# Cross attention and a mixture of experts on one core: two batches normed together at the start, a shorter tile table, and new instruction orders

## What is computed

```python
def _L0_xattn_ref(q, k, v):                       # q: (16, 128, 256), k = v: (16, 128, 64)
    qh = q.reshape(B, S, KV, G, D).transpose(0, 2, 3, 1, 4)
    ...
    scores = jnp.einsum('bkgsd,bktd->bkgst', qh, kh) / scale
    weights = jax.nn.softmax(scores, axis=-1)
    out = jnp.einsum('bkgst,bktd->bkgsd', weights, vh)
...
def _L0_ffn_ref(x, gate_w, w1, w2, w3):
    scores = jnp.einsum('ti,ei->te', xt, gate_w)
    probs = jax.nn.softmax(scores, axis=-1)
    expert_weights, expert_indices = jax.lax.top_k(probs, NUM_ACT)
    expert_weights = expert_weights / expert_weights.sum(axis=-1, keepdims=True)
    x1 = jax.nn.silu(jnp.einsum('ti,eoi->teo', xt, w1))
    x3 = jnp.einsum('ti,eoi->teo', xt, w3)
    expert_outs_all = jnp.einsum('teo,eio->tei', x1 * x3, w2)
    ...
x = x + _L0_xattn_ref(_layernorm(x, axis=-1), ctx_512, ctx_512)
x = x + _L0_ffn_ref(_layernorm(x, axis=-1), gate_w, w1, w2, w3)
```

## Time and profile before

| | |
|---|---|
| three executions | 444.84, 445.28 and 445.86 us, median 445.28 |
| the profiled execution | 443.68 us, of it the span 441.8 us |
| granted TensorE clock, mean | 0.943 of full speed |
| busy TensorE / VectorE / ScalarE / POOL | 355.9 / 233.6 / 196.7 / 183.6 us |
| moved by DMA | 51.16 MB, 116 GB/s over the span |
| chain that ended last | TensorE 53%, DMA 16%, VectorE 8%, issue 8%, POOL 8% |

### The profile page before, as it was taken

One profiled execution on the slowest core, in us unless ns is written; L12 is line 12 of the kernel. 1 busy time (PEld: TensorE's weight loads), 2 busy tenths in 40 slices (PEclk: granted clock), 3 DMA queues, 4 the chain that ended last, 5 costly groups with the idle time before them and its releaser, 6 DMA issues.

```text
span 441.8 us, 8620 instructions
## 1 busy us (share of the span) xinstructions
PE 355.9 (81%) x2255; PEld 255.9 (58%) x2256; DVE 233.6 (53%) x659; ACT 196.7 (45%) x397; POOL 183.6 (42%) x361
## 2 busy tenths in 40 slices
PE   0177878798888879833059999999999999999991
PEld 0054444455445445222038888888888888888870
DVE  6777786888787776558943222233232222333320
ACT  3325768686777657859022223222222332322220
POOL 6662263377655746476301232322222332222232
PEclk9989999999999998975559999999999999999997
DMA  6676798968876785853412333333333333333222
GB/s 204 148 156 128 216 222 202 225 151 208 202 180 183 185 218 165 282 170 107 144 48 37 61 50 49 48 50 57 48 51 57 48 48 48 52 54 48 36 24 24
DMA packets 46209, 51.16 MB, mean 116 GB/s; under 512 B 18659, under 2 KB 39267, under 8 KB 46179
## 3 DMA queue, kind: packets, MB, share of 16 engines
q1 hardware_dynamic: 37299, 39.64, 35.3%
q0 software_dynamic: 7152, 9.34, 13.5%
q10 hardware_dynamic: 1728, 1.82, 1.3%
HBM read 31.51 MB, written 16.69 MB: 109 GB/s over the span
## 4 chain that ended last, share of the span: by engine, by line
PE 53%; DMA 16%; DVE 8%; issue 8%; POOL 8%; SPq 3%; ACT 2%; POOLq 1%; ACTq 0%
PE bank L898 25%; PE bank L916 15%; DMA qst<-negT 10%; PE bank L908 4%; DVE wlo L1306 3%; POOL slots_d L545 3%; DMA rows<-rows 2%; PE bank L886 2%; PE bank L720 2%; PE bank L697 1%; SPq L315 1%; DMA qst<-qparts_d 1%; PE bank L694 1%; POOL x L516 1%; PE bank L733 1%
## 5 line engine op out<-in xcount | busy, mean ns | idle before, releaser
L660 POOL DMA_INDIRECT out_rows<-ys,meta x39 | 60.9, 1561 | 155.6 <-DVE ys L1537 145.3
L1251 DVE TENSOR_REDUCE negm<-bank 128x4 f32<-128x512 f32 x128 | 83.9, 680 | 25.0 <-PE bank L697 23.5
L1530 DVE TENSOR_TENSOR gat<-bank,sil 128x512 f32<-128x512 f32 x39 | 27.0, 692 | 112.8 <-PE bank L898 112.8
L967 ACT ACTIVATE prob<-bank 128x512 f32<-128x512 f32 x128 | 73.1, 597 | 26.7 <-PE bank L720 23.6
L916 PE MATMUL bank<-w,gT 128*128 x312 | 73.9, 380 | 0.8 <-ACT gT L1171 0.8
L1165 ACT ACTIVATE sil<-bank 128x512 f32<-128x512 f32 x39 | 23.3, 597 | 105.9 <-PE bank L898 105.9
L720 PE MATMUL bank<-qst,kst 128*128 128x512 bf16 x128 | 49.0, 387 | 20.8 <-DMA qst<-negT 18.8
L898 PE MATMUL bank<-whi,xhi 128*128 x156 | 60.3, 468 | 1.2 <-ACT xhi L1159 1.2
L916 PEld LDWEIGHTS bank<-w,gT 128*128 128x128 f32 x312 | 56.3, 190 | 7.1 <-issue 1.0
L697 PEld LDWEIGHTS bank<-kst,qst 125*128 125x128 bf16 x512 | 41.5, 102 | 23.3 <-issue 2.8
L697 PE MATMUL bank<-kst,qst 125*128 125x128 bf16 x512 | 51.8, 227 | 0.0
(11 more groups left out here) (121 smaller groups left out, 474.5 us busy)
## 6 DMA issues: line engine op xcount, KB each, us to landing
xs<-slots_d SPq DMA_DIRECT2D x39, 129.0 KB, 2.0
w<-in_w1T SPq DMA_DIRECT2D x8, 512.0 KB
w<-in_w3T SPq DMA_DIRECT2D x8, 512.0 KB
w<-in_w2T SPq DMA_DIRECT2D x8, 512.0 KB
qparts_d<-qp SPq DMA_DIRECT2D x16, 192.0 KB, 4.9
qst<-qparts_d SPq DMA_DIRECT2D x16, 192.0 KB
qst<-qparts_d SPq DMA_DIRECT2D x16, 128.0 KB
vblk<-in_v SPq DMA_DIRECT2D x16, 128.0 KB
```

What stands on the lines that cost most here:

```text
L660: pool.indirect_dma_start(out, IndirectOffsetOnAxis(ap=meta[:, r4, 0:1].bitcast(I32), axis=0), ys[:, r4, :], None, compute_op=ALU.add).the ...
L967: act.activation(prob[:, k, :], ps_e[k % 2][:, :], ACT.Exp, scale=SCALE).then_inc(exp_done, 1)
L1251: dve.tensor_reduce(negm[:, b % 2, g * G:(g + 1) * G], ps_s[(8 * b + g) % 3][:, :].rearrange("p (h t) -> p h t", h=G), AX.X, ALU.max, nega ...
L1530: dve.tensor_tensor(gat[:, u, :], ps_h3[u][:, :], sil, ALU.mult).then_inc(g_done, 1)
```

## The change

- `GROUPS` becomes (0, 2), (2, 4), (4, 8), (8, 12), (12, 16): batches 0 and 1 share the first root, of two columns.
- The table of tiles counts in rows in place of tiles. It has 12 steps: two steps of 39 columns are gone and one of 8 columns is new. `row0` is ready two steps before the end, and SP waits for it alone (`ROW0`); ScalarE does not wait for the table any more.
- `place(8)` is ahead of the table instead of behind it.
- The spare padding (two DMAs) is sent by SP in round -1.
- The first score group of a batch goes out one slot earlier, at the end of the round before.
- All steps of all engines stand in new orders. Of these: `neg_transpose` goes behind the fourth exponent product (and in odd rounds behind `pv`); `root_unit` goes from the head of odd rounds to the end of even ones on POOL; `normal1` of odd rounds' ends goes to even rounds on ScalarE; w2 is loaded in rounds 14 and 15 (two pieces each) and after the loop (four), before two in each of rounds 12 to 15; POOL forms remainder 5 instead of 2.

```diff
-GROUPS = [(0, 1), (1, 4), (4, 8), (8, 12), (12, 16)]
+GROUPS = [(0, 2), (2, 4), (4, 8), (8, 12), (12, 16)]
...
-    c[:, C_TILE:C_TILE + NT] = np.arange(NT)
+    c[:, C_TILE:C_TILE + NT] = np.arange(NT) * P
...
+            def pad_spare():
+                sp.wait_ge(pad_row, 3)
+                sp.dma_start(out[T:T + P, :], pad[:, 0:D]).then_inc(pads_out, 16)
+                sp.dma_start(slots_d[E * REGION:E * REGION + P, :], pad[:, :]).then_inc(pads_out, 16)
...
-            sp.wait_ge(table, TABLE)
+            sp.wait_ge(table, ROW0)
...
                 if i % 2 == 0 and 0 <= i + 2 < B:
                     neg_split(i + 2, 3)
+                if i % 2 == 0 and 0 <= i - 2 < B - 2:
+                    root_unit((i - 2) // 2)
...
+            put_tokens(6)
+            root_unit(7)
             add_res(15)
...
             pad_experts(act, 1)
-            act.wait_ge(table, TABLE)
...
             pad_rows()
+            place(8)
...
-            link(dve.tensor_scalar(cnti[:, 1, :], cnti[:, 0, :], 7, None, ALU.arith_shift_right))
+            link(dve.tensor_scalar(cnti[:, 1, :], cnti[:, 0, :], -P, None, ALU.bitwise_and))
...
+            link(dve.tensor_scalar(nx[:, :], ntl[:, :], -1.0, float(REGION), ALU.mult, ALU.add))
+            link(dve.tensor_tensor(gn[:, :, :], ge[:, :, :], nx[:, None, :].broadcast_to(bc), ALU.mult))
+            link(dve.tensor_reduce(ta[:, :], gn[:, :, :], AX.X, ALU.add))
+            link(dve.tensor_tensor(ta[:, :], ta[:, :], first_rows, ALU.add))
+            link(dve.tensor_scalar(row0[:, :], ta[:, :], float(E * REGION), None, ALU.min))
             link(dve.tensor_reduce(te[:, :], ge[:, :, :], AX.X, ALU.add))
-            link(dve.tensor_reduce(tx[:, :], gn[:, :, :], AX.X, ALU.add))
-            link(dve.tensor_tensor(tx[:, :], tiles, tx[:, :], ALU.subtract))
-            link(dve.tensor_scalar(ta[:, :], te[:, :], float(REGION), None, ALU.mult))
-            link(dve.scalar_tensor_tensor(ta[:, :], tx[:, :], float(P), ta[:, :], ALU.mult, ALU.add))
-            link(dve.tensor_scalar(row0[:, :], ta[:, :], float(E * REGION), None, ALU.min))
             link(dve.tensor_scalar(texp[:, :], te[:, :], float(E - 1), None, ALU.min))
-            place(8)
```

More of the change, by code:

```diff
@@ L379, in _ @@
                     stack_q(i + 3)
-                if i % 2 == 1 and 2 <= i + 3 < B:
-                    stack_q(i + 3)
-                if i % 2 == 1 and 0 <= i - 2 < B:
-                    store_x2(i - 2)
+                if i == 4:
+                    load_w13(8)
+                if i % 2 == 0 and 0 <= i + 1 < B:
+                    lay_neg(i + 1)
+                if i == 9:
+                    load_w13(13)
+                if i % 2 == 0 and 0 <= i + 1 < B:
+                    load_v(i + 1)
@@ L384, in _ @@
+                if i % 2 == 0 and 3 <= i + 4 < B:
+                    write_q(i + 4)
+                if i == 14:
+                    load_w2(0)
                 if i % 2 == 1 and 0 <= i + 1 < B:
                     lay_neg(i + 1)
-                if i % 2 == 0 and 0 <= i + 1 < B:
-                    lay_neg(i + 1)
+                if i == 3:
+                    load_w13(5)
+                if i == 12:
+                    load_w13(15)
+                if i % 2 == 0 and 8 <= i < B:
+                    load_res(i)
@@ L388, in _ @@
+                if i == 10:
+                    load_w13(14)
+                if i == 5:
+                    load_w13(10)
+                if i % 2 == 0 and 8 <= i + 1 < B:
+                    load_res(i + 1)
+                if i == 6:
+                    load_w13(11)
+                if i == 2:
+                    load_w13(3)
                 if i % 2 == 1 and 3 <= i + 4 < B:
                     write_q(i + 4)
-                if i % 2 == 0 and 3 <= i + 4 < B:
-                    write_q(i + 4)
@@ L402, in _ @@
+                if i % 2 == 1 and 0 <= i - 1 < B:
+                    store_x2(i - 1)
+                if i % 2 == 0 and 0 <= i - 4 < B - 2:
+                    copy_rows((i - 4) // 2)
+                if i == 15:
+                    load_w2(2)
+                if i == 14:
+                    load_w2(1)
+                if i == 2:
+                    load_w13(4)
+                if i % 2 == 0 and 2 <= i + 4 < B:
+                    load_k(i + 4)
                 if i == 3:
                     load_w13(6)
-                if i == 2:
-                    load_w13(4)
@@ L446, in _ @@
-                if i == 8:
-                    load_w13(13)
+                if i % 2 == 0 and 0 <= i - 1 < B:
+                    store_x2(i - 1)
+            load_w2(4)
             copy_rows(6)
+            load_w2(5)
             store_x2(15)
             copy_rows(7)
+            load_w2(6)
+            load_w2(7)
             copy_rows(8)
-            sp.wait_ge(pad_row, 3)
-            sp.dma_start(out[T:T + P, :], pad[:, 0:D]).then_inc(pads_out, 16)
-            sp.dma_start(slots_d[E * REGION:E * REGION + P, :], pad[:, :]).then_inc(pads_out, 16)
@@ L632, in _ @@
                 if i % 2 == 1 and 0 <= i + 2 < B:
+                    neg_split(i + 2, 0)
+                if i % 2 == 1 and 0 <= i + 2 < B:
                     neg_split(i + 2, 1)
-                if i == 15:
-                    put_tokens(7)
+                if i % 2 == 1 and 0 <= i + 2 < B:
+                    neg_split(i + 2, 2)
                 if i % 2 == 0 and 0 <= i + 2 < B:
@@ L1115, in _ @@
                 if i >= 0:
+                    exps(i, 6)
+                if i == 5:
+                    split_hi(4)
+                if i == 2:
+                    split_hi(1)
+                if i >= 0:
                     exps(i, 7)
+                if i == 4:
+                    split_hi(3)
                 if i % 2 == 1 and 0 <= i - 3 < B - 2:
                     copy_x2T((i - 3) // 2)
[L1119 to L1124 removed]
+            split_hi(10)
             split_hi(11)
@@ L1421, in _ @@
                     normalise(i - 1, 1)
-                if 8 * i + 21 < KV * B:
-                    maxima(8 * i + 21)
-                if i == 15:
-                    split_lo(8)
+                if i % 2 == 0 and 3 <= i + 5 < B:
+                    q_residual1(i + 5)
+                if i % 2 == 0 and 0 <= i - 4 < B - 2:
+                    mark((i - 4) // 2)
                 if 8 * i + 22 < KV * B:
```

392 lines of the change are left out of this document (171 added, 221 removed).

## The result

| | before | with the change |
|---|---|---|
| median, runs | 445.06 us, 4 runs (441.68 to 445.86) | 448.69 us, 4 runs (446.61 to 450.49) |
| the profiled execution | 443.68 us, span 441.8 | 447.88 us, span 446.0 |
| granted TensorE clock, mean | 0.943 | 0.935 |

Ratio 1.010, 95% interval 1.0065 to 1.0135: the change makes the kernel slower by 1%, some 4.5 us. The forecast was 444.0 and faster. The ratios and their intervals leave out executions that took over 1.5% longer than the fastest of the same kernel.

The account below looks back on a forecast made before the run. No engine fills the loop, where TensorE waits longest for the negated maxima's DMA; VectorE bounds the bridge, TensorE the tiles. Start -0.2, loop +0.7, bridge -1.8 sum to -1.3 us: 444.0 us from the 445.28 median, forecast's own range 442 to 444.4.

Parts of the forecast that it names:

- Start, -0.2: Start up to batch 0's first exponent product at 37.70 us: net 0.2 us earlier, ends -2.2 and +0.8.
- at once: Start: batch 1, normed at 16.43 before, would be normed directly behind batch 0; 2.2 us if all arrives.
- SP sends it before the stacking, as before: Start: K's remainder now waits on batch 1's residual, but keeps its place on SP, so batch 0's stacking changes little.
- Loop, +0.7: Attention loop: later transpose of the maxima +2.7, POOL waits gone -2.0; ends -3.6 and +5.4 us.
- the 2.7 taken: Loop: half of the later transpose's full +5.4 us, since a transfer sent later may land at the same time.
- The POOL waits: Loop: the maxima transpose's two waits on POOL, 2.0 us, should go as unit roots move.
- wrong if the wait on `qst<-negT` is far from 18.8: Sign for the loop term: TensorE's wait for the DMA laying negated maxima into `qst` should stay near 18.8 us.
- Bridge, -1.8: Between loop and expert tiles: token write -0.2, fewer remainders -1.8, unit 6's weights +0.5, shorter table -0.24; ends -2.8 and 0.
- the 0.2 of the token write: Bridge: POOL's token write ahead of batch 15's residual moves behind it, -0.2 us.
- the cover: Bridge: VectorE's work hides the scatters and the four w2 loads sent there, two before the last row copy.
- Padding, 0: Spare padding at the slots' end leaves SP early; it stood behind row copies whose scatters come later anyway: 0.
- the loop gives it back: Rival, slower: latency from issue stays, the moved transpose lengthens 11 cycles by 5.4 us; 446.7 to 448.7 us, chance 0.33.

## Why the prediction was wrong

- **Start, -0.2, measured +2.55 at the first product and 3.9 in the whole: the step that failed.** It moved batch 1's norm up "at once" and priced the group of two columns as the group of one. The rows then read had both a memset at 13.98 and a norm at 16.43, not the rows of the roots between. There two steps of three columns took 0.58 and 1.04 us where their neighbours took 0.16, the first ending with a `tensor_tensor` of POOL (13.26 to 13.92), the second with the memset (13.98 to 15.78). That was the sign that VectorE is held beside POOL. The Trainium skill, SBUF — State Buffer, section on who interferes with whom, has the rule: a `tensor_scalar` in a two-port mode and a GpSimd instruction exclude each other, and the later one is fully blocked. The rows agree (two columns 1.82 us, one column 0.15 beside the same memset), and each time it was VectorE that was held; which mode a step ran in, no trace shows. No rival of the prediction had it. With one-column steps the store of batch 1 left at 18.10 (forecast 18.0), its stacking at 23.32 (22.3), and the first product came at 37.61 (37.5): the rest of the start's term came out nearly as forecast. "SP sends it before the stacking, as before" was true in order and wrong in time: K's remainder, held with VectorE, took SP's queue and the stacking of batch 0 from 16.25 to 19.54. The store of batch 1, forecast at 18.0, left at 20.75, its stacking, forecast at 22.3, at 25.80. The two steps of before:

```profile
13.36 0.58 DVE L1234 TENSOR_SCALAR rs<-rs 128x3 f32<-128x3 f32 x1
...
14.77 1.04 DVE L1234 TENSOR_SCALAR rs<-rs 128x3 f32<-128x3 f32 x1
```

- **Loop, +0.7, measured +2.6 (first to last product).** The later transpose costs +1.0 alone (-0.7 to 2.7), so the 2.7 taken is the upper edge, and the reason given for it, that the transfer may land at the same time, is not what its trace shows (6.0 us from issue to product, before 6.4). The POOL waits went from 2.0 to 1.2, not to 0. The forecast "wrong if the wait on `qst<-negT` is far from 18.8" came true: 3.0. What was missing is the price of the early group in the loop, which was costed in the start only (0.74). It moved the wait to the stacking. Alone on before it costs 4.6 us; inside the change its price is not settled. The first five batches also run at a mean clock of 0.93 instead of 1.00, which no term held. And the shift of addresses, worth some 2.9 us, was in the change's new tensor `nx` and in no term.
- **Bridge, -1.8, measured -1.4: right in mechanism by the traces.** From the statistics (205.89) to the counts (215.93) it took 10.04 us instead of 11.32: -1.3, the forecast's -1.8 + 0.5. The table gave 0.1 instead of 0.24, two of its steps being held beside POOL's scatters, which `place(8)`, priced at 0, sends during it; the 0.2 of the token write lie ahead of this stretch. The 14 remainders stand directly behind the table, and the cover held: the first tile waits for `wlo` alone.
- **Padding, 0: right** (0.9987, interval 0.9944 to 1.003).
- **Sum.** Stalls 3.9, addresses 2.9, bridge -1.4 make +5.4 us against some 4.5 measured; the rest of the loop's order is then -1 in sum, but the first two terms are each uncertain by some 2 us, so this sum is no proof. The rival "the loop gives it back" had the right time (446.7 to 448.7) by luck: its price, 5.4 us for the later transpose, is excluded by the run with that transpose alone, though its premise, a latency unchanged from issue, is not. The forecast took 0.2% as what a measurement can tell; with 12 executions the intervals came out at 0.3 to 0.5% to either side.

## What to carry to other kernels

Before widening or moving a small VectorE step, look at what POOL does at that very moment, and at the durations of its neighbours: a 0.16 us step that once takes 0.58 or 1.04 us is being held by a neighbour, and one more column can put the critical path behind a whole memset. When a wait is removed from an in-order queue, name the instruction that now stands first in it and the transfer that it needs; and read the granted clock behind each long wait of TensorE, since such a wait may be paid twice. Treat a changed buffer size as an edit of its own, and test it with the addresses held fixed.

## What the runs showed of the hardware

- One `tensor_scalar` of two fp32 or int32 columns in SBUF is held to the end of a concurrent GpSimd memset (1.82 against 0.17 us); the same work as two one-column instructions is not (0.21 us for both), which is cheaper than the stall and nearly as cheap as one instruction.
- Moving the SBUF tensors behind one buffer (`w13`, `qst`, `prob`, `kst` and `xin` among them) by 128 bytes, with no instruction changed, cost 0.65% (1.0016 to 1.0114); moves by 32 and 64 bytes cost nothing measurable. The starts 0, 32 and 224 bytes past a multiple of 256 are alike, 160 is slow, and why is open.
- A wait of TensorE of 3.3 us was followed by more than 3 us at half clock in the middle of a busy loop.
